# Edge loop of a graph network kernel: three of four quads have their clips spread between VectorE's PSUM copies

## What is computed

```
npj = relu(layer_norm(x @ Wp + bp))                       # 20 values per node
kron = einsum('ea,ek->eak', npj[src], npj[dst])           # 400 per edge
kron = relu(layer_norm(kron @ Wk + bk))                   # 256 per edge
kron_feat = segment_sum(kron, dst)
logits = relu(concat(x[dst], x[src]) @ We + be)
a = softmax of the logits over the edges of a node
context = relu(segment_sum((x @ Wn + bn)[src] * a, dst))
```

## Time and profile before

| | |
|---|---|
| median of 3 runs | 8942.02 us |
| the profiled execution | 8936.67 us |
| its span in the trace | 8935.2 us |
| TensorE busy | 6445.6 us (72%) |
| VectorE busy | 5818.1 us (65%) |
| ScalarE busy | 3738.4 us (42%) |
| GpSimd busy | 4539.2 us (51%) |
| granted TensorE clock, mean | 0.879 of full speed |
| edge loop, first to last products | 4652.8 to 8211.8 us |

### The profile page before, as it was taken

One profiled execution on the slowest core, in us unless ns is written; L12 is line 12 of the kernel. 1 busy time (PEld: TensorE's weight loads), 2 busy tenths in 40 slices (PEclk: granted clock), 3 DMA queues, 4 the chain that ended last, 5 costly groups with the idle time before them and its releaser, 6 DMA issues.

```text
span 8935.2 us, 169603 instructions
## 1 busy us (share of the span) xinstructions
PE 6445.6 (72%) x32727; PEld 4098.9 (46%) x32728; DVE 5818.1 (65%) x16429; ACT 3738.4 (42%) x10876; POOL 4539.2 (51%) x4743
## 2 busy tenths in 40 slices
PE   3244666666666699987767777777777777777888
PEld 2221444444444477763334444444444444444444
DVE  8896444444444466665547778777777777776666
ACT  0000444444444300003336666666666666665433
POOL 0000777777778500000017777777777777775100
PEclk9676777877787799996669999999999999999998
DMA  0002333333322388865557877777877888776200
GB/s 13 0 0 75 94 99 100 99 99 99 100 97 95 118 263 262 263 229 226 223 221 213 214 213 215 214 214 212 215 214 213 214 215 215 211 216 182 59 19 18
DMA packets 973553, 1399.03 MB, mean 157 GB/s; under 512 B 378858, under 2 KB 744924, under 8 KB 960328
## 3 DMA queue, kind: packets, MB, share of 16 engines
q1 hardware_dynamic: 761663, 797.51, 29.6%
q0 software_dynamic: 208448, 596.38, 23.6%
q10 hardware_dynamic: 3012, 1.51, 0.1%
HBM read 986.32 MB, written 415.51 MB: 157 GB/s over the span
## 4 chain that ended last, share of the span: by engine, by line
PE 31%; issue 18%; DVE 18%; DMA 12%; SPq 8%; ACT 7%; POOL 4%; DVEq 2%; ACTq 1%; POOLq 0%
DMA arena_n<-rec_dram 8%; SPq L550 7%; PE ps L1991 6%; PE ps L1889 5%; PE ps L1786 4%; PE ps L2009 3%; ACT junk L993 3%; POOL msg_dram L814 3%; PE ps L2000 3%; DMA arena_e<-msg_dram 2%; DVE arena_e L1635 2%; PE ps L1904 2%; DVE arena_r L1297 2%; DVE arena_e L1575 2%; ACT L1014 1%
## 5 line engine op out<-in xcount | busy, mean ns | idle before, releaser
L835 POOL DMA_INDIRECT arena_n<-tab_dram,idxs x2624 | 2744.4, 1046 | 2374.1 <-DVE idxs L1550 1575.3
L1991 PE MATMUL ps<-arena_n 126*128 126x257 f32 x5234 | 1677.5, 417 | 582.7 <-DVE arena_e L1575 562.7
L814 POOL DMA_INDIRECT msg_dram<-arena_e,idxq x1616 | 1634.8, 1012 | 434.3 <-issue 425.2
L1991 PEld LDWEIGHTS ps<-arena_n 126*128 126x128 f32 x5234 | 841.8, 193 | 1144.8 <-DVE arena_e L1575 1005.3
L1878 PE MATMUL ps<-arena_n,arena_r 128*128 x3232 | 1096.1, 498 | 354.8 <-ACT arena_r L902 354.8
L1575 DVE COPY arena_e<-ps 128x257 f32<-128x257 f32 x1962 | 815.0, 421 | 528.3 <-ACT junk L993 514.6
L1635 DVE SCALAR_TENSOR_TENSOR arena_e<-arena_e,rstd,nbetak_b 128x256 f32<-128x256 f32 x2608 | 1088.3, 480 | 31.6 <-DVE rstd L1641 31.1
L993 ACT ACTIVATE junk<-ps 128x256 f32<-128x256 f32 x2617 | 985.3, 382 | 203.5 <-PE ps L1991 188.6
L1878 PEld LDWEIGHTS ps<-arena_n,arena_r 128*128 128x128 f32 x3232 | 758.7, 246 | 595.7 <-issue 466.9
L907 ACT ACTIVATE arena_e<-ps,recq 128x256 f32<-128x256 f32 x1616 | 739.3, 475 | 662.6 <-PE ps L1878 653.9
L1889 PE MATMUL ps<-arena_e,oh 128*128 128x256 f32 x3520 | 816.7, 387 | 88.3 <-DVE oh L1351 86.8
(11 more groups left out here) (333 smaller groups left out, 9126.7 us busy)
## 6 DMA issues: line engine op xcount, KB each, us to landing
arena_n<-m_dram SPq DMA_DIRECT2D x2624, 126.5 KB
arena_e<-msg_dram SPq DMA_DIRECT2D x441, 514.0 KB, 4.4
m_dram<-arena_e SPq DMA_DIRECT2D x49, 1413.5 KB, 4.9
m_dram<-arena_e SPq DMA_DIRECT2D x49, 1285.0 KB, 4.5
arena_n<-tab_dram,idxs POOLq DMA_INDIRECT x2624
hist_dram<-arena_r SPq DMA_DIRECT2D x163, 253.0 KB
arena_n<-rec_dram SPq DMA_DIRECT2D x1616, 2.0 KB
msg_dram<-arena_e,idxq POOLq DMA_INDIRECT x1616
```

Of the source, the lines that this page charges most:

```text
L814: nc.gpsimd.indirect_dma_start(out=msg_dram, in_=msgs[:, u, j, :], in_offset=None, out_offset=bass.IndirectOffsetOnAxis(ap=idxq[:, u, j:j ...
L835: nc.gpsimd.indirect_dma_start(out=feat[:, u, i, :], out_offset=None, in_=tab_dram, in_offset=bass.IndirectOffsetOnAxis(ap=idxs[:, u, i:i ...
L1991: mm(ps[:, bank_of(i), 0:HC], prods_t[0:KM, s % 2, j * P:(j + 1) * P], m_ring[0:KM, i, :], start=True, stop=True).then_inc(e_h, 1)
```

## The change

`clipped` takes the tiles it shall clip. In quads with s > 0 (once there is a group before), clip 0 is issued behind copy 0, clip 1 behind copy 1, clip 2 behind the products and in front of copy 2, and clip 3 where all four stood. The quad s = 0, in which the reciprocals are made, keeps its four clips in a row at the end.

```diff
-            def clipped(g, u, s):
-                if s == 0:
+            def clipped(g, u, s, part=range(G)):
+                if s == 0 and part[0] == 0:
                     dve.wait_ge(e_rs, g + 1)
                     all_copied(g)
-                for j in range(G):
+                for j in part:
...
                     one, two, three = (earlier(it, main, n) for n in (1, 2, 3))
+                    spread = one is not None and s > 0
                     copied(main, 0)
+                    if spread:
+                        clipped(*one, s, (0,))
                     copied(main, 1)
+                    if spread:
+                        clipped(*one, s, (1,))
...
                     products(here, it)
+                    if spread:
+                        clipped(*one, s, (2,))
                     copied(main, 2)
...
-                        clipped(*one, s)
+                        clipped(*one, s, (3,) if spread else range(G))
```

## The result

The changed kernel takes **9195.17 us** (median of 4 runs, 9181.6 to 9199.21), the kernel before in the same comparison 8944.99 us. The ratio is 1.0278, 95% interval [1.0259, 1.0296]: 2.8% slower. The forecast was 9188 us with a range of 9080 to 9290.

What follows compares the result with a forecast made beforehand. Waits bound the edge loop: PSUM copy, product, square and next copy form a ring over three engines. Terms of 19.6, 95.9, 73.7 and 57.1 us sum to +246: 9183 us, plus 5.3 for the median, 9188; range 9080 to 9290.

Steps and rivals of the forecast that it cites:

- Clip 0 ahead of copy 1, quad 1: Quad 0 to 1: copy 1 starts 0.12 us later per group, with 0.20 us of wait filled; 19.6 us in all.
- Clips 1 and 2 ahead of copy 2, quad 1: Quad 1 to 2: the 2.81 us chain behind copy 2 is no longer covered, +0.62 us, with a 1.0 us wait.
- The same in quad 2: Quad 2 to 3: later copy 2 and the 2.81 us chain, +0.58 us, with a new wait of about 0.6 us.
- Context sums in quad 3: Quad 3 to 0: weighted one-hots move by 0.80 us and TensorE's context sums wait for them, +0.35 us per group.
- Quad 0: Quad 0 keeps its clips and its copy 2 is not moved; no cost was counted.
- The branch: Every fourth group, 40 crossings: quad 1 to 2 costs 0.49 us in place of 0.62, quad 2 to 3 0.06.
- low bound: Whole kernel: about +150 us, with quad 1 to 2 and 2 to 3 at 0.4 us each, quad 3 at 0.12.
- gap rival: VectorE's waits at copy 1 are filled and the chain has slack: -98 us, 8844 us; chance 0.05.
- GpSimd rival: Edge loop: GpSimd's gathers set the pace, the ring has slack and the time stays at 8942 us; chance 0.05.
- clock rival: Edge loop: TensorE's clock falls to its lower level in every group, +167 us more, 9355 us; chance 0.07.
- Theories B and C: Formed after the measurement: B, clips ahead make products or one-hots late; C, VectorE loses time going between copies and clips.
- A: Theory formed after the measurement, the ring: copy 2 is late, and the chain behind it is no longer covered.

Runs made afterwards that it cites:

- clip 0 only: Against the changed kernel, only clip 0 stays ahead, between copies 0 and 1; clips 1 to 3 stand behind copy 2 again; 11178 us.

## Why the prediction was right

The copies 1 give each step (predicted, then measured over the groups away from the branch). Such a group takes 22.26 us (6063.51 to 6085.77); 22.4 were predicted.

1. **Clip 0 ahead of copy 1, quad 1:** +0.12; measured +0.10 (5.60 to 5.70). The wait of 0.20 us was filled, and the rest of the clip showed.
2. **Clips 1 and 2 ahead of copy 2, quad 1:** +0.62 with a wait of 1.0 behind; measured +0.53 (4.88 to 5.41) with a wait of 0.94. Copy 1 to copy 2 went up by 0.79, nearly as predicted (0.80); the term that was off is the chain, 2.73 us where 2.81 was added. The 2.81 was read rightly: with copy 2 in its old place and nothing else in the way the chain takes that long (the run with clips moved out of quad 2). With copy 2 later, product 1's weights go in 0.48 us behind its start in place of 0.55, and the whole is 0.08 shorter. The clipped sums start on TensorE at the same moment as copy 2 in the old order (6022.66 and 6022.68); that they make the difference is likely, and not shown.
3. **The same in quad 2:** +0.58 with a wait of 0.6; measured +0.50 (4.15 to 4.65) with a wait of 0.41. The same 0.08 us; the wait is shorter than predicted because clip 0 of quad 3 takes 0.39 of it. With the change in quads 1 and 2 only the wait is 0.81.
4. **Context sums in quad 3:** +0.35; measured +0.40 (6.09 to 6.49). The mechanism is in the rows: L2016 starts 0.83 us behind L2007, with the weighted one-hots as its releaser. The half change in quad 3 alone gives the same 6.48.
5. **Quad 0:** copy 1 to copy 2 is 1.98 us in both traces, as said.
6. **The branch:** here the sum was right by two errors. Step 2 was put at +0.49 at the crossing and step 3 at +0.06 behind it. Measured +0.60 (7.89 to 8.49) and +0.36 (5.16 to 5.52). The step that failed is "product 1 runs late already": the 5.51 us to the copy at 6051.37 was one crossing, where the mean over all of them is 5.16, so the chain had less to hide behind. And in the group behind the one that crosses, quad 1 to 2 takes 5.90 and not 5.41, which no step foresaw. The 8.44 us to which the prediction added was one crossing, too; their mean is 7.89. And the time does not come the way it was told, by clips on VectorE's own path: VectorE reaches the branch 0.40 us earlier than before (3.50 us behind copy 1 of quad 1 in place of 3.90, as means), and the idle time there grows from 2.71 to 3.70. What ends it no row names. Part of the 0.60 may not be the clips' at all, since the crossing also takes 8.14 us with the change in quad 3 only and with `sum_slots` moved, where nothing near it on VectorE was changed. The mean of quad 1 to 2 is thus +0.66 where steps 2 and 6 gave 0.59, and that of quad 2 to 3 is +0.46 as against 0.45.

The sum predicted was 246 us; the profiled executions differ by 244.9 us (9181.6 and 8936.7). The loop itself lost 258, and 13 us of scatter came back outside it. So the mechanism is right, and that the total is right to a few us is luck: it is closer than its parts. The low bound was also added up a little short: with 0.4 for steps 2 and 3 and 0.12 for step 4, and the rest as in the sum, it is about 160 us, not 150.

The **gap rival** (8844 us) needed a product 1 that is held by something else than copy 2. In quad 1 this was so before, for a little: its weights went in 0.73 us behind copy 2's start (6018.57), right behind a turn that had waited for ScalarE's exponentials, and with no wait for the copy:

```profile
6019.16 0.14 PEld L1786 LDWEIGHTS ps<-ident,arena_n 128*128 128x128 f32 x1 [1.22 <-issue]
6019.30 0.30 PEld L1991 LDWEIGHTS ps<-arena_n 126*128 126x128 f32 x2
```

That was 0.25 us of slack (a chain of 2.98 in place of 2.73), which is why a copy 2 later by 0.79 cost 0.53. In the trace of after the weights go in 0.48 us behind copy 2's start with the copy as their releaser, in both quads. The 0.20 us at quad 1 was filled, and the distance still grew by 0.10; the 0.40 at quad 2 became 0.94.

The rule of the Trainium skill that was weighed (Perfetto Trace Analysis, Optimization Strategy) holds in the reading that asks what ends a gap; the moved `sum_slots` is that reading put to use, the chain that ends the gap of 2.41 us at quad 0 runs through TensorE, and what stood in its way there was worth 1.1%.

The **GpSimd rival** was wrong in its result: the changed kernel's GpSimd waits for TensorE's buffers, so the ring has no slack. But its row was truer than the prediction granted: GpSimd had no idle time beyond 0.30 us per gather before either, and has none in the faster version. What it lacked was the question how far ahead the gathers are: at least 13 us from group 20 on in the kernel before, so a full GpSimd was not its bound.

The **clock rival** did not happen: 0.97 in the stage.

Theories B and C, formed afterwards, have rows against them: a clip takes 479 ns as before and VectorE's busy time does not rise, which leaves C no place; `products` wait for nothing new, TensorE's turn follows product 1 without a wait (only L1793's releasers L1016 and L1625 of before appear), and with quads 1 and 2 alone the loss sits exactly behind their copies 2. The one-hots are late in quad 3, as step 4 says; that part of B is A's own fourth step. The runs that were to part A from B and C fell in sets of over 11000 us. So it was not told by a time, but by the undisturbed groups in them: 4.25, 4.65 and 5.04 us for one, two and three clips ahead.

## What to carry to other kernels

When one engine has small gaps, look at what ends them before filling them: in a ring over several engines, work put ahead of the instruction that releases the next engine delays the release in full (here 0.79 us for two clips), and what exceeds the slack there becomes time (0.5 us). The same work behind that instruction was almost free, as cover of the 2.7 us chain. When the releasing instruction is moved ahead instead, look for the next one that takes its place (here, by the timing, the products). Price a half change by the chain it starts, not by the other half, since the costs of two halves do not add (194 and 140 us against 250). And the gap worth attacking is the longest one, from the side of the engine that ends it: moving two matmul pairs off the chain gained 1.1% where filling 0.6 us of gaps lost 2.8%. And an engine without idle time is not the bound while its results lie ready long before their use: measure the lead, as with the gathers.

## What the runs showed of the hardware

- The same kernel takes 8940 us in some sets of runs and 11204 to 11376 us in others, on one and the same chip, too. A set can be steady in itself: 8930.5 to 8949.8 us in 13 runs, 11167.9 to 11240.5 in 15. The difference is not spread evenly. The first row below is of the kernel before, the second of "clip 0 only" (11178 us), as GB/s in 40 slices of each span:

```profile
GB/s 13 0 0 75 94 99 100 99 99 99 100 97 95 118 263 262 263 229 226 223 221 213 214 213 215 214 214 212 215 214 213 214 215 215 211 216 182 59 19 18
```

```profile
GB/s 11 0 37 85 81 82 81 79 82 82 81 83 135 262 264 239 221 224 167 142 142 144 141 144 140 143 143 144 144 139 138 142 143 143 144 138 144 115 19 18
```

  The stage that moves 263 GB/s does so in both. The stages with many small packets fall from 100 to 82 and from 214 to 143 GB/s. A kernel whose loads are just in time on one occasion can be paced by them on another, and the order of its arithmetic then hardly shows (0.99 to 1.01 for all orders tried).
- At the loop's branch VectorE idles 2.71 us in the mean of 38 crossings of the kernel before (1.90 to 3.94) and 3.70 us in the changed one (2.96 to 4.30), which reaches the branch earlier. One crossing, such as the 3.39 us of the earlier trace rows, is a poor base for a sum. The group behind the crossing is disturbed, too: quad 1 to 2 took 5.90 us there, 0.49 more than in the other groups of the changed kernel.
- GpSimd's gathers follow each other at 0.30 us with a mean length of 1046 ns in one kernel and 1018 in two others, at the same median of 0.95 us: 23% of them last over 1.1 us in the kernel before, 14 to 16% in the other two.
